# Down-sampling matmuls in four quarters of 32 columns in place of two halves of 64, in a filtered leaky ReLU kernel

## What is computed

```python
# layer 0: a sine of a plane wave, one for each channel, is added to both batch images
lin = jnp.einsum('oc,chw->ohw', W, coord) + b[:, None, None]
x = x + jnp.sin(lin)[None]
# layer 1: bias, up-sampling by 2, leaky ReLU, down-sampling by 2
out = x + bias[None, :, None, None]
out = _sep_upfirdn(out, up_filter * 2, 2, 1, UP_PAD)      # 12 taps, rows and columns: 512 x 512
out = leaky_relu(out, 0.2) * sqrt(2)
out = _sep_upfirdn(out, down_filter, 1, 2, DOWN_PAD)      # 12 taps: back to 256 x 256
```

## Time and profile before

| what | value |
|---|---|
| median of three runs | 6847.44 us |
| the profiled execution's own time | 6846.66 us |
| its span, first to last instruction | 6844.9 us |
| mean granted clock of TensorE | 1.000 of full speed |
| TensorE streams (PE) busy | 6782.4 us, 99% of the span |
| TensorE weight loads (PEld) busy | 6303.4 us, 92% |
| ScalarE busy | 4084.0 us, 60% |
| VectorE busy | 3954.3 us, 58% |
| GpSimd busy | 1296.0 us, 19% |
| DMA | 82 GB/s over the span |

### The profile page before, as it was taken

One profiled execution on the slowest core, in us unless ns is written; L12 is line 12 of the kernel. 1 busy time (PEld: TensorE's weight loads), 2 busy tenths in 40 slices (PEclk: granted clock), 3 DMA queues, 4 the chain that ended last, 5 costly groups with the idle time before them and its releaser, 6 DMA issues.

```text
span 6844.9 us, 361569 instructions
## 1 busy us (share of the span) xinstructions
PE 6782.4 (99%) x148480; PEld 6303.4 (92%) x148480; DVE 3954.3 (58%) x6218; ACT 4084.0 (60%) x7688; POOL 1296.0 (19%) x1041
## 2 busy tenths in 40 slices
PE   6999999999999999999999999999999999999999
PEld 6999999999999999999999999999999999999998
DVE  6555555555555555555555555555555555555555
ACT  4566566655666665566566656656665665666555
POOL 2111111111111111111111111111111111111111
PEclk9999999999999999999999999999999999999999
DMA  3222222222222222222222222222222222222222
GB/s 116 81 81 81 80 81 81 81 81 81 80 80 81 81 80 81 81 81 81 80 81 81 81 81 81 80 80 81 81 80 81 81 81 80 80 81 81 81 81 74
DMA packets 580065, 558.27 MB, mean 82 GB/s; under 512 B 40400, under 2 KB 574928, under 8 KB 580048
## 3 DMA queue, kind: packets, MB, share of 16 engines
q1 hardware_dynamic: 580048, 558.02, 25.8%
HBM read 278.94 MB, written 278.92 MB: 82 GB/s over the span
## 4 chain that ended last, share of the span: by engine, by line
PE 99%; DVE 1%; issue 0%; DMA 0%; ACT 0%; SPq 0%; DVEq 0%
PE y_ps L450 34%; PE p_ps L434 34%; PE o_ps L434 15%; PE a_ps L450 14%; PE o_ps L460 3%; DVE up_band L377 0%; DVE angle L354 0%; DVE angle L352 0%; DVE phase L344 0%; ACT trig L258 0%; DVE trig_parts L361 0%; DVE angle L356 0%; DVE turns L348 0%; DVE turns L350 0%; DVE trig_parts L360 0%
## 5 line engine op out<-in xcount | busy, mean ns | idle before, releaser
L392 DVE SCALAR_TENSOR_TENSOR z<-y_ps,leak 128x512 f32<-128x512 f32 x4096 | 2716.1, 684 | 1522.9 <-ACT leak L278 1522.9
L278 ACT ACTIVATE leak<-y_ps 128x512 f32<-128x512 f32 x4096 | 2245.3, 605 | 1024.0 <-PE y_ps L450 1024.0
L450 PE MATMUL y_ps<-up_band,a_sb 64*128 64x138 f32 (+2 forms) x32768 | 2807.5, 288 | 1.6 <-ACT a_sb L271 1.5
L434 PE MATMUL p_ps<-down_band,z 128*64 128x68 f32 (+1 forms) x65536 | 2445.9, 227 | 1.8 <-DVE z L392 1.0
L434 PEld LDWEIGHTS p_ps<-down_band,z 128*64 128x64 f32 x65536 | 2156.2, 137 | 267.3 <-DVE z L392 1.3
L450 PEld LDWEIGHTS y_ps<-up_band,a_sb 64*128 64x128 f32 x32768 | 2228.7, 186 | 148.7 <-issue 1.8
L245 POOL TENSOR_TENSOR x_sum<-x_raw,f_sb 128x512 f32<-128x512 f32 x1024 | 1283.6, 1281 | 5514.0 <-ACT f_sb L264 5504.6
L400 DVE COPY p_rows<-p_ps 128x512 f32<-128x512 f32 x2048 | 1411.0, 689 | 1350.4 <-PE p_ps L434 1277.0
L271 ACT COPY a_sb<-a_ps 128x512 f32<-128x512 f32 x2048 | 1100.3, 589 | 1179.8 <-PE a_ps L450 1179.8
L450 PE MATMUL a_ps<-up_band,x_sum 64*128 64x138 f32 (+2 forms) x16384 | 1297.0, 275 | 26.7 <-POOL x_sum L245 26.6
L434 PE MATMUL o_ps<-down_band,p_rows 128*64 128x68 f32 (+1 forms) x32768 | 1171.0, 224 | 0.7 <-issue 0.7
(11 more groups left out here) (28 smaller groups left out, 40.7 us busy)
## 6 DMA issues: line engine op xcount, KB each, us to landing
x_raw<-in_x_dram SPq DMA_DIRECT2D x1024, 256.0 KB, 2.7
out_dram<-o_out SPq DMA_DIRECT2D x1024, 256.0 KB, 2.1
f_rows<-trig_dram SPq DMA_DIRECT2D x512, 20.0 KB
trig_dram<-trig_parts SPq DMA_DIRECT2D x32, 256.0 KB, 2.5
trig_dram<-ones SPq DMA_DIRECT2D x4, 256.0 KB, 2.3
trig_dram<-bias_wide SPq DMA_DIRECT2D x4, 256.0 KB, 2.5
up_taps<-in_L_conv_up_filter_dram SPq DMA_DIRECT2D x1, 6.0 KB, 2.3
down_taps<-_L_conv_down_filter_dram SPq DMA_DIRECT2D x1, 6.0 KB, 2.4
```

The costliest lines, as they stand in the source:

```text
L278: nc.scalar.mul(leak[i % 2][:, :], y_ps[i][:, :], SLOPE * GAIN).then_inc(leak_done, 1)
L392: nc.vector.scalar_tensor_tensor(z[n][:, i, :], y_ps[i][:, :], GAIN, leak[i % 2][:, :], ALU.mult, ALU.max).then_inc(z_done, 1)
L434: last = nc.tensor.matmul(out_ps[half * HALF:(half + 1) * HALF, lo:hi], data[:, t, col:col + HALF], down_band[:, band:band + hi - lo], sta ...
L450: last = nc.tensor.matmul(outs[o][:, lo:hi], data[row, k, (at + o) * P:(at + o + 1) * P], up_band[row, band:band + hi - lo], start=step == ...
```

## The change

`down` splits its stationary operand into four quarters of 32 columns, each with its output in 32 PSUM partitions of its own. A call is then 4 bands by 4 quarters, 16 matmuls, and 64 instructions of TensorE. The loop of TensorE holds one channel, two slots, in place of two channels.

```diff
-    PE_CHANNELS = 2
+    PE_CHANNELS = 1
     assert (C - 2) % PE_CHANNELS == 0
...
             def down(data, out_ps, at, first):
 
                 for t, (lo, hi, band) in enumerate(DN_SPAN):
-                    for half in range(2):
-                        col = at + half * HALF
-                        last = nc.tensor.matmul(out_ps[half * HALF:(half + 1) * HALF, lo:hi],
-                                                data[:, t, col:col + HALF], down_band[:, band:band + hi - lo],
+                    for quarter in range(0, P, P // 4):
+                        col = at + quarter
+                        last = nc.tensor.matmul(out_ps[quarter:quarter + P // 4, lo:hi],
+                                                data[:, t, col:col + P // 4], down_band[:, band:band + hi - lo],
                                                 start=first and t == 0, stop=t == len(DN_SPAN) - 1,
                                                 skip_group_check=True)
                 return last
```

## The result

The changed kernel takes 6956.57 us (median of four runs, 6955.34 to 6957.79) against 6846.91 us before: a ratio of 1.016, 95% interval 1.0143 to 1.0178. It is 110 us slower, and the time lies outside the range of the prediction (6808 to 6925 us). The forecast of 6823 us was wrong. Rival 1 names the right mechanism, but its size was too small: the upper end of 6945 us is 12 us short, its middle of 6904 us is 53 us short.

What follows compares the result with a forecast made beforehand. The prediction took TensorE's own instruction sequence, busy 99% of the span, as the bound. From 6846.66 us it took 25 us for weight loads, other terms nothing: 6822, so 6823 us as median, range 6808 to 6925 us.

Steps and rivals of the forecast that it cites:

- Rival 1: Sequencer stays 34 instructions ahead, so its work shows at the loop's end and ahead of o_ps: 6904 us; 28%.
- Streaming: Down-sampling groups: four tiles run side by side, so a round (streams running at once) stays 60.6 ns; gains nothing.
- Rival 2: Down-sampling streams: four tiles don't run at full rate, so a 0.97 us group becomes 1.94; 9830 us; 9%.
- Weight loads: At each switch from up- to down-sampling, a shorter bare load minus later last-tile start nets 12 ns, 25 us in all.
- Feeding: Sequencer filling TensorE's queue in down-sampling groups: 128 instructions in 0.97 us, 7.6 ns each, keeps up; no cost.
- straight parts: Written-out code outside the loop: about 384 more instructions a channel, some 7 packets more to fetch; no cost.
- Cover: Sequencer's work at the loop's end and ahead of o_ps stays hidden under 68 queued instructions, 0.52 us; no cost.
- The loop: TensorE's loop body goes from 1160 to 964 instructions and is not fetched again; 508 branches cost nothing while covered.

Runs made afterwards that it cites:

- p0_quarters: Kernel before, with quarters only in the first half of down_rows, halves elsewhere and two channels in the loop: 6833.21 us, ratio 0.9979.
- best version: Changed kernel with down_cols' waits and loop border moved ahead of a slot's last up_cols, quarters only in the loop, halves in written-out channels: 6821.53 us, ratio 0.9963.
- quarters_two: Changed kernel with two channels in TensorE's loop in place of one, quarters kept: 9395.35 us, ratio 1.3715.

## Why the prediction was wrong

**Streaming: right.** Four tiles stream side by side; a round stays at 60.6 ns and o_ps at 0.97 us. Rival 2 (9830 us) is out. The streams of the four tiles of a round start 6 to 7 ns apart in the changed kernel, so the floor of 25 ns that rival 2 quotes does not hold between tiles.

**Weight loads: right.** The longest stream record of p_ps is 250 ns where it was 275, 25 ns less as worked out. The net gain is 13 ns a switch in p0_quarters, and 0.053 us for four switches in the best version; 12 ns and 0.048 us were forecast. The 6823 us of the forecast is close to the time of the version in which the sequencer's work stays hidden and the written-out channels keep their halves, 6821.5 us.

**Feeding: right in the loop, wrong outside it.** The sequencer feeds 7.6 ns an instruction in the loop. In the written-out channels the program arrives more slowly, and the "no cost" of the straight parts was 7 us (4 more packets in the run, where some 7 were forecast).

**Cover: this step failed.** The sentence was "I take it that each array tile has its own queue", and from it 68 instructions ahead. At the loop's end the number is 34 with one tile, 34 with two and 28 with four, at each of the 508 ends (254 in the kernel before). So the sequencer's work outlasted what was queued: 0.18 us a channel at the loop's end and 0.07 us ahead of o_ps, where the prediction had put nothing. The inference went from streams of two tiles that start 7 ns apart to separate queues. At most the starts show that the array does not keep strictly to the program's order; they say nothing of queues, and there was no second row for it. The row on hand, 34, would have fitted a shared queue just as well, as rival 1 said, and the chances went the other way. The Trainium skill (Advanced Engine Details and Errata, section Engine Queue Depths) gives TensorE 64 entries, "complicated with tiling"; the prediction made of it a share of 16 for each tile, so 64 with four tiles. The trace disagrees with that reading, with 28, and no run here shows 64.

**The size of rival 1.** With 28 ahead in place of 34, the loop's end cost 0.18 us and not 0.12, and o_ps 0.07 and not 0.04: 91 + 36 us against 61 + 20. Six instructions of 7.6 ns are 0.05 us, which is most of the difference. The written-out channels added 7.

**The loop.** That its body would not be fetched again was right for 964 instructions, and two runs bound the edge: 1464 stay (p0_quarters), 1976 don't (quarters_two). The Trainium skill, Runtime: NRT & Kernel Launch, section Instruction fetch mechanics, gives TensorE room for 2048 instructions in blocks of 256. The blocks agree with the packets of 16 KB. A body of 1976 should have fitted in that room and did not; why is open, since no run here has a body between 1464 and 1976.

## What to carry to other kernels

When instructions get shorter, count what stood hidden behind them: a queue that runs ahead by a number of instructions covers half the time when each lasts half as long. On an engine that is busy 99% of the span, look at the sequencer's own work (branch, register arithmetic, waits that passed long ago; here about 0.1 us each, and 0.27 us from the branch to what follows it) and put it where long instructions are in the queue, or where a semaphore holds the sequencer anyway; a cut into smaller tiles is judged only after that. And check that a loop's body, grown by the cut, is still kept on the engine.

## What the runs showed that I had not expected

- The sequencer is 34 instructions ahead of the array at the loop's end with one or two tiles in the down-sampling groups, and 28 with four; it is 28 in the up-sampling groups of the kernel before too.
- The written-out program is fetched in packets mostly 3.6 to 4.4 us apart, of 256 instructions each, so short instructions outside a loop are limited by fetch: 3.4 us of idle TensorE in the 50 us from 69 us on.
- A loop body of 1976 instructions is fetched in 10 packets a round and costs 5 us a channel, a part of it at the lower clock; one of 1464 is not fetched again.
